# A twelve-sublayer decoder: the end of the first mixture of experts moved into the stages of the block behind it, and the opening transfers staged

## The reference, cut to what matters

```python
x = _layernorm(x + _L0_attn_ref(x, gate_w, gate_b, w1, b1, w2, b2))       # 8 experts, top 2, gelu, 128 -> 512 -> 128
x = _layernorm(x + _L0_xattn_ref(x, ctx_1024, Wq, bq, Wk, bk, Wv, bv))    # one head, keys and values from ctx
x = _layernorm(x + _L0_ffn_ref(x, W1, b1, W2, b2))                        # weights rounded to -1, 0 or 1, 128 -> 512 -> 128
...
```

## Time and profile before

| | us |
|---|---|
| median of 3 runs | 3722.18 (3711.93 to 3723.31) |
| the profiled execution | 3689.48 |
| its span, first to last instruction | 3687.8 |
| PE busy | 2935.0 (80%) |
| DVE busy | 2176.2 (59%) |
| ACT busy | 1819.6 (49%) |
| POOL busy | 1825.7 (50%) |
| mean granted TensorE clock | 0.895 |

### The profile page before, as it was taken

One profiled execution on the slowest core, in us unless ns is written; L12 is line 12 of the kernel. 1 busy time (PEld: TensorE's weight loads), 2 busy tenths in 40 slices (PEclk: granted clock), 3 DMA queues, 4 the chain that ended last, 5 costly groups with the idle time before them and its releaser, 6 DMA issues. The chain is left out here.

```text
span 3687.8 us, 83881 instructions
## 1 busy us (share of the span) xinstructions
PE 2935.0 (80%) x28814; PEld 2040.0 (55%) x28814; DVE 2176.2 (59%) x5986; ACT 1819.6 (49%) x3516; POOL 1825.7 (50%) x1735
## 2 busy tenths in 40 slices
PE   2688873998888789963529997997999869995895
PEld 1677762775555556642315664664444536664784
DVE  2111133756878668863247886877898678884124
ACT  0333331844555556630216665776466677662342
POOL 3533254434777645526465554664033655553335
PEclk9998986999999889985559998998999889996997
DMA  8566652120010121114621112221000011222675
GB/s 284 160 184 182 185 161 70 45 8 25 30 46 37 41 74 70 71 45 118 169 57 51 58 54 85 77 90 62 1 1 1 1 30 56 72 69 84 204 218 149
DMA packets 325000, 315.45 MB, mean 86 GB/s; under 512 B 111316, under 2 KB 244853, under 8 KB 324472
## 3 DMA queue, kind: packets, MB, share of 16 engines
q1 hardware_dynamic: 283080, 261.98, 23.4%
q0 software_dynamic: 16384, 33.59, 3.1%
q10 hardware_dynamic: 25264, 16.40, 1.5%
HBM read 167.28 MB, written 60.69 MB: 62 GB/s over the span
## 5 line engine op out<-in xcount | busy, mean ns | idle before, releaser
L1054 PE MATMUL moe_first_out_ps<-moe_first_expert_w,moe_first_hid 128*128 128x128 f32 x1360 | 214.9, 311 | 84.5 <-ACT moe_first_hid L1098 63.5
L1098 ACT ACTIVATE moe_first_hid<-moe_first_hid_ps,moe_first_expert_w 128x256 f32<-128x256 f32 x340 | 139.0, 472 | 260.2 <-PE moe_first_hid_ps L1043 141.7
L908 DVE TENSOR_TENSOR moe_first_tile_y<-moe_first_out_ps,moe_first_expert_w 128x256 f32<-128x256 f32 x85 | 36.1, 425 | 368.9 <-PE moe_first_out_ps L1054 187.7
L1054 PEld LDWEIGHTS moe_first_out_ps<-moe_first_expert_w,moe_first_hid 128*128 128x128 f32 x1360 | 191.4, 211 | 102.9 <-issue 42.3
L1117 POOL DMA_INDIRECT slot_x<-x_tok,moe_first_slots x128 | 124.6, 974 | 119.7 <-DMA slot_x<-blank 49.3
L1131 POOL DMA_INDIRECT moe_first_token_y<-slot_y,moe_first_slots x128 | 123.5, 965 | 107.9 <-issue 67.8
L1043 PE MATMUL moe_first_hid_ps<-moe_first_tile_xT,moe_first_expert_w 128*128 128x256 f32 x680 | 171.4, 397 | 1.9 <-issue 1.4
L1813 POOL TENSOR_TENSOR causal_k_blocks<-causal_k_T,headmask 128x1024 f32<-128x1024 f32 x64 | 121.3, 1898 | 99.4 <-PE causal_scores L1423 93.7
L1813 POOL TENSOR_TENSOR alibi_k_blocks<-alibi_k_T,headmask 128x1024 f32<-128x1024 f32 x64 | 121.3, 1897 | 94.0 <-PE alibi_scores L1423 90.0
L1813 POOL TENSOR_TENSOR full_k_blocks<-full_k_T,headmask 128x1024 f32<-128x1024 f32 x64 | 120.8, 1898 | 83.7 <-PE full_scores L1423 78.8
L1098 ACT ACTIVATE moe_last_hid<-moe_last_hid_ps,moe_last_expert_w 128x256 f32<-128x256 f32 x212 | 86.7, 471 | 140.2 <-PE moe_last_hid_ps L1043 110.0
(11 more groups left out here) (561 smaller groups left out, 8902.0 us busy)
## 6 DMA issues: line engine op xcount, KB each, us to landing
moe_first_expert_w<-in_L_attn_experts SPq DMA_DIRECT2D x85, 578.0 KB
moe_last_expert_w<-in_L_ffn_experts SPq DMA_DIRECT2D x53, 578.0 KB
moe_first_tile_x<-slot_x SPq DMA_DIRECT2D x85, 128.0 KB
slot_y<-moe_first_tile_y SPq DMA_DIRECT2D x85, 128.0 KB
slot_x<-blank ACTq DMA_DIRECT2D x2, 4992.0 KB, 35.9
L_ffn_tile_x<-slot_x SPq DMA_DIRECT2D x32, 256.0 KB
slot_y<-L_ffn_tile_y SPq DMA_DIRECT2D x32, 256.0 KB
moe_last_tile_x<-slot_x SPq DMA_DIRECT2D x53, 128.0 KB
```

Of the source, the lines that this page charges most:

```text
L908: dve.tensor_tensor(y_out[:, q, :, :], out_bank[q][:, 0:SLOT_TILE].rearrange("p (s d) -> p s d", s=SPAN), over(wall[:, j % RING, 2 * FF + ...
L1054: last = pe.matmul(out_bank[j % 2][:, D * s:D * s + D], hid[:, j % 2, b, TILE * s:TILE * s + TILE], wall[:, j % RING, FF + D * b:FF + D * ...
L1098: act.activation(hid[:, j % 2, b, :], hid_bank[b // 2][:, SLOT_TILE * (b % 2):SLOT_TILE * (b % 2) + SLOT_TILE], gelu, bias=wall[:, j % RIN ...
```

## The change

Two things are done.

**The opening.** `SLOT_TILES` becomes (23, 39, 39), so that the first part's slot tensor has 23 tiles, which that part needs; `L_ffn` takes the two of 39 instead. `x_T` and `x_tok` are loaded in three pieces of 16, 32 and 16 tiles, each piece of both forms together, and SP holds back the second and third until slot tensor 0 is cleared. ACT clears slot tensor 0 first, and 1 and 2 each after the exponential of the part before and once that piece of `x_T` has landed.

**The end of the first sublayer.** With `hand_over` the `moe` generator closes its block after the last `evict`, keeps `slots`, `weights`, `token_y` and the tail's buffers, and hands a `Late` object to `chained`. The chunks 12 to 15 (m = 0 to 3) are gathered, summed, normalised, transposed and copied in stages of the joined block, one chunk to three steps. The clearing of the first sublayer's semaphores moves behind the joined block; one barrier stays between the blocks.

```diff
-SLOT_TILES = (39, 39, 23)
+SLOT_TILES = (23, 39, 39)
+LOAD_TILES = (16, 32, 16)
...
+        for n, tiles in enumerate(LOAD_TILES):
+            some, cols = slice(first, first + tiles), slice(TILE * first, TILE * (first + tiles))
+            if n == 1 and hold_for_clearing:
+                sp.wait_ge(self.cleared[0], 16)
+            sp.dma_start(self.x_T[:, cols], self.dram["x_T"][:, cols]).then_inc(self.T_loaded[n], 16)
+            sp.dma_start(self.x_tok[:, some, :], rows[:, some, :]).then_inc(self.tok_loaded[n], 16)
+            first += tiles
...
@@ moe, ACT
                 if net.at == 0:
                     net.await_columns(act, 0)
-                    net.clear_slots(act)
+                    net.clear_slots(act, 0)
...
+                    if net.at == 0 and part + 1 < parts:
+                        net.await_columns(act, part + 1)
+                        net.clear_slots(act, part + 1)
...
@@ moe, the block's end
-        late = chunks[-1]
+        last_chunks = chunks[-1]
+        late = [] if hand_over else last_chunks
...
+        def late_gpsimd(pool):
+            def rows(c):
+                m, third = divmod(c, 3)
+                if m < len(last_chunks):
+                    gather(pool, FIRST + m, ((0, 1), (2,), (3,))[third])
+            def inverse_std(c):
+                m, third = divmod(c, 3)
+                if third == 0 and m < len(last_chunks):
+                    tail.inverse_std(pool, FIRST + m)
+            return [(-5, rows), (-1, inverse_std)]
...
+            return [(-2, weighted_sum), (0, normalise)]
...
+                    if m:
+                        pe.wait_ge(host.xT_copied, c - 2)
+                    tail.transpose(pe, FIRST + m, bank)
+            return [(0, transpose)]
...
+                    tail.copy_transposed(act, FIRST + m, bank)
+            return [(0, copy)]
...
@@ single_head
+                if before and c >= before.first:
+                    pe.wait_ge(before.tail.xT_copied, c + 1)
...
+            def turn_normed(c):
+                if before:
+                    pe.wait_ge(before.tail.xT_copied, before.copied_by(c + 3))
+                tail.transpose(pe, c, xT_bank)
...
+                if before and c >= before.first:
+                    pool.wait_ge(before.tail.normed, c + 1)
```

More of the change, by code:

```diff
@@ L40 @@
 LN_EPS = 1e-5
[L41 removed]
+IN_CHAIN = (2, 3, 10)
 BIG = 3.0e38
@@ L150, in __init__, with load_stream @@
         self.sublayer_sems = []
-    def load_stream(self, sp):
-        half, tiles = TOKENS // 2, TILES // 2
-        for n in range(2):
-            sp.dma_start(self.x_T[:, half * n:half * n + half], self.dram["x_T"][:, half * n:half * n + half])\
-                .then_inc(self.T_loaded[n], 16)
-        rows = self.dram["x"].rearrange("(t p) d -> p t d", p=128)
-        for n in range(2):
-            sp.dma_start(self.x_tok[:, tiles * n:tiles * n + tiles, :], rows[:, tiles * n:tiles * n + tiles, :])\
-                .then_inc(self.tok_loaded[n], 16)
+    def load_stream(self, sp, hold_for_clearing=False):
+        rows = self.dram["x"].rearrange("(t p) d -> p t d", p=128)
+        first = 0
+        for n, tiles in enumerate(LOAD_TILES):
[5 more added lines that the diff above has]
+            first += tiles
     def load_constants(self, sp):
@@ L684, in moe @@
     tile_of = [(n, m) for n, count in enumerate(NTS) for m in range(count)]
-    def halves(part):
-        half = TILES // 2
-        return range(origin[part] // half, (origin[part] + sizes[part] - 1) // half + 1)
     def by_expert(t, k):
@@ L767, in moe, with combine, gather @@
         after_tile = {due(c): c for c in range(CHUNKS) if due(c) is not None}
-        late = chunks[-1]
+        last_chunks = chunks[-1]
+        late = [] if hand_over else last_chunks
+        def combine(dve, c):
+            p, part = c % 2, part_of[c]
+            dve.wait_ge(gathered[p], 16 * PER * top * (c // 2 + 1))
+            if c >= 2:
+                dve.wait_ge(tail.normed, c - 1)
+            for r in range(top):
+                if r:
+                    dve.wait_ge(half_summed, c + 1)
+                for k in range(PER):
+                    t = PER * c + k - origin[part]
+                    base_row = net.x_tok[:, PER * c + k, :] if r == 0 else tail.r[:, p, k, :]
+                    last = dve.scalar_tensor_tensor(tail.r[:, p, k, :], y_in[:, p, k, r, :], weights[:, part, r, t:t + 1],
+                                                    base_row, ALU.mult, ALU.add)
+                last.then_inc(tail.summed if r == top - 1 else half_summed, 1)
+            tail.moments(dve, c)
+        def gather(pool, c, some):
+            p, part = c % 2, part_of[c]
+            if c == chunks[part][0] and 0 in some:
+                for q in range(2):
+                    pool.wait_ge(y_stored[q], 16 * ((reach[part + 1] + 1 - q) // 2))
+            if c >= 2 and 0 in some:
+                pool.wait_ge(tail.summed, c - 1)
+            for k in some:
+                for r in range(top):
+                    t = PER * c + k - origin[part]
+                    pool.indirect_dma_start(y_in[:, p, k, r, :], None, slot_y[part][0:NTS[part] * SLOT_TILE, :],
+                                            bass.IndirectOffsetOnAxis(slots[:, part, r, t:t + 1], 0))\
+                        .then_inc(gathered[p], 16)
         with nc.Block() as block:
@@ L1004, in route @@
                 def route(part):
-                    for n in halves(part):
-                        net.await_columns(pe, n)
+                    net.await_columns(pe, part)
                     if part:
@@ L1143, in _ @@
                     pool.wait_ge(net.cleared[part], 16)
-                    for n in halves(part):
-                        net.await_rows(pool, n)
+                    net.await_rows(pool, part)
                     pool.wait_ge(planned, 2 * part + 2)
@@ L1916, in finish, with __init__, copied_by @@
     tail.all_stored(sp)
+class Late:
+    def __init__(self, tail, first, vector, tensor, scalar, gpsimd):
+        self.tail, self.first = tail, first
+        self.vector, self.tensor, self.scalar, self.gpsimd = vector, tensor, scalar, gpsimd
+    def copied_by(self, step):
+        return self.first + min(CHUNKS - self.first, max(0, (step + 2) // 3))
 class Flow:
@@ L1937, in chained @@
     yield
-    flows = [next(sublayers[0])]
+    late = next(giver) if giver else None
+    if giver:
+        net.nc.all_engine_barrier()
+        net.at += 1
+    flows = [sublayers[0].send(late) if giver else next(sublayers[0])]
     for sublayer in sublayers[1:]:
@@ L1949, in _ @@
         def _(dve):
-            staged(joined(flows[0].vector(dve), flows[1].vector(dve)), AHEAD, BEHIND)
+            staged(joined(flows[0].vector(dve), flows[1].vector(dve)) + (late.vector(dve) if late else []), AHEAD, BEHIND)
         @block.sync
```

128 lines of the change are left out of this document (67 added, 61 removed).

## The result

| | before | with the change |
|---|---|---|
| median (8 runs each) | 3717.06 us (3700.65 to 3734.51) | 3686.22 us (3679.78 to 3694.07) |
| ratio | 1 | 0.9921, 95% interval 0.9906 to 0.9936 |
| the profiled execution | 3689.48 us | 3685.81 us |

The change saves about 29 us by the ratio and 31 by the two medians; the forecast was 56, with a range of 3642 to 3696. So the tiles are compared with the second profile.

A forecast was written before the change was run, and what follows sets the result against it. It took two meeting opening chains (POOL's scatters, PE's late routing) and one chain at the first sublayer's end as bounds. Opening 27 plus end 29 (55 less 26 given back) made 56: 3722.2 - 56 = 3666 us, range 3642 to 3696.

The forecast's parts named there:

- the rule weighed: Joined block's gathers: DVE's two-port mode could lock POOL from writing descriptors, 68 us lost, total near 3734; not adopted.
- its routing takes 7 us: Opening: the second piece of `x_T` lands at about 31 us and PE then routes that part in 7 us.
- nothing in the trace tells what causes the drag: Opening: PE's unexplained slow third routing, 24.6 us before; kept or gone, first turn 19.7 or 33.7 us earlier, middle 27.
- the slower rival: Opening: second routing drags beside POOL's scatters, 0.65 us per instruction, first turn at about 298, time 3885; chance 0.04.
- can be turned at about 72: Opening, chain of POOL's scatters: first slot tile fetched at 69.2 us, turned at about 72, 33.7 us earlier.
- the clearing of slot tensor 2 costed at nothing: Opening: its rest may be in flight at the first tiles, 5 MB in 15 us, ending by about 75; no cost.
- the delays add: Joined block: PE's and POOL's delays do not overlap, 45 us given back instead of 26, time 3685; chance 0.12.
- Start: Joined block: first maxima come 16.6 us after its start instead of 11.8, giving back 5 us.
- never idle: Joined block, steps 1 to 6: POOL always busy, some 6.9 us a step, giving back 12 us.
- PE's stands: Joined block, steps 3, 6, 9: PE waits 4 to 5 us at late transposes; two counted half, 7 us given back.
- POOL held up by DVE: Joined block: each of 32 gathers 0.41 us slower, 13 us more given back, 43 in all, time 3679; chance 0.06.
- The opening gains nothing: Opening: drag starts sooner or second routing is delayed and drags, first turn stays at 105, time 3693; chance 0.06.

The follow-up runs named there:

- the second profile: The kernel before, unchanged, run and profiled again on the first kind of chip: 3712.86 us, profiled span 3711.1 us.
- change_again: The change, unchanged, timed again on a chip of the second kind: 3502.45 us, ratio 0.9905 to the kernel before on that chip.
- before_third: The kernel before, unchanged, profiled again on a chip of the second kind: 3541.14 us.

## Why the prediction was right or wrong

**Right**: faster, and inside the range. The time is less close than it looks: the gain is half of the forecast's 56, 3686 lies outside the forecast's own range of 3650 to 3680, and 5 us of the way come from the first median of the kernel before (3722 from 3 runs, 3717 from 8). The own range takes 22 us for the end at its lowest where its terms say 10; with 10 it would have reached 3692. The first scatter at 27 (27.3). The slot tiles unchanged. Gathers at 0.94 to 1.18 us in the joined block, where the kernel before has up to 1.156: they were not slowed, so the rule weighed (the Trainium skill, SBUF — State Buffer, section "SBUF: two separate sides") has no row here either. The joined block's earlier start, 55.0 forecast, is 59.3: it starts 1.6 us behind the last bias, not 5.6.

**The opening, 27 forecast, 10.6 measured.** The step that failed is "its routing takes 7 us". It took 43.4 in the change's profile on the first kind of chip. I had refused to name a cause of the drag ("nothing in the trace tells what causes the drag") and costed the second routing at full pace all the same, though the change puts it beside POOL's scatters; the slower rival had just this mechanism. It was priced far too high, since the drag ends with POOL's scatters, and does not run on for each instruction. The trace of before hinted at it. Behind the 32nd scatter at 90.27, the last in the earlier trace rows, POOL issues four of the second part, and the dragging matmuls stop 2.9 us behind the last of them, at 98.22:

```profile
95.33 0.96 POOL L1117 DMA_INDIRECT slot_x<-x_tok,moe_first_slots  x1 [0.30 <-issue]
```

On the second kind of chip "7 us" was exact (7.00), and another step failed: "can be turned at about 72" and the clearing of slot tensor 2 costed at nothing. It is issued from 43.45 on and lands at 84.4. From 50 to 80 us the DMA share is 1.05, that is all 16 engines are busy, and the rows that the first tile needs lie behind it. The last of its 32 scatters, the fetch of its rows and its turn in `change_again`:

```profile
67.09 0.96 POOL L1132 DMA_INDIRECT slot_x<-x_tok,moe_first_slots  x1 [0.30 <-issue]
...
73.60 0.39 SPq L987 DMA_DIRECT2D moe_first_tile_x<-slot_x  x1
...
79.83 0.69 PE L1044 MATMUL moe_first_turn_ps<-ident,moe_first_tile_x 128*128 128x128 f32 x2 [19.85 <-DMA moe_first_tile_x<-slot_x]
```

From scatter to fetch are 6.5 us and from fetch to turn 6.2. In `before_third`, whose clearings have landed by then, both are 2.3 (90.99, 93.24, 95.49). That makes the turn at 79.8 instead of 72: 7.8 us that the forecast did not have. There is no drag to remove from the kernel before there, so its first turn is at 95.5.

**The end, 29 forecast, 14.4 measured.** The give-back is 44.9 instead of 26, which is the rival "the delays add" (45). That rival's time, 3685, is nearly the measured one, but that is luck: it has the opening at 27. By the terms of the end, on the first kind of chip:
- Start: 5 forecast, 9.6 measured. On the second kind it is 5.9; DVE's late start is the rest.
- POOL "never idle": wrong. It waits 34.1 us for DVE. Half of the gathers, left out, took 7.2 us out of the steps, where I had 12 for POOL's whole load; so the size may be near, and the path is another: it runs over POOL's late inverse deviation to DVE's normalising and PE's transposes.
- PE's stands: 7 forecast for them (two halves and one whole of "4 to 5 us" are 8 to 10), "POOL is late anyway, so I count half". They do not lie in POOL's shadow. The three long steps have 15.5, 14.4 and 11.5 us, 26 us over three steps of 5.1 together, and spreading the stages and a bank of their own took 9.5 and 8.8 us out of the steps. The cause is a chain: PE's last item of a step waits for rows of that same step, DVE normalises them only behind POOL's inverse deviation, and the late transposes share a bank with the attention's.

**The rivals**: "POOL held up by DVE" fell. "The opening gains nothing" was half right, with the drag sooner; the opening still gained 10 us.

## What to carry to other kernels

Work that is moved into another loop's steps needs a whole step of distance from its producer on every engine and a buffer (here a PSUM bank) of its own; with both given, POOL's added load is the smaller part of what it cost. (Of 41.0 us given back, distance took away 16.1 and the bank 8.8, so that at most 16 are left for POOL. In the close spacing half of its gathers was worth 13, since their time lay on the same chain.) A stall that the trace gives no reason for is not a number to be carried over: look at what the other engines do from its first to its last instruction, and do not put new work there. And a transfer that is "still in flight" is not free when the first thing that is waited for moves by the same DMA engines.

## What was not expected of the hardware

- On one kind of chip PE and DVE start instructions late while POOL issues indirect transfers one after another: pairs of routing matmuls 1.4 to 2.8 us apart, DVE's ready maxima 9.5 us late, slot tiles at 476.1 us instead of 363.1. On two other chips the same program shows nothing of it, and takes 180 us less. Between the chips most of this difference (113 us) lies in the 85 slot tiles. The drag does not begin with the transfers: 45 and 71 routing matmuls ran at full pace beside POOL's scatters before it set in. Each chip was used in one set of runs only, so it is not shown that the chip itself makes the kind, and not something else that held at the time.
- Which path of POOL's transfers the two kinds differ in stays open; no run could tell it. The profile's list of DMA queues has two that carry instructions (packets of 0.01 and 0.02 MB). In the change's profile on the first kind none of their packets falls between 36 and 80 us, and three do on the second kind, but engines that start fewer instructions need fewer, so that is no proof. The Trainium skill (Runtime: NRT & Kernel Launch, section "Instruction fetch mechanics") says that the engines' instructions are fetched ahead in blocks and that the cost of this is mostly hidden; the drag would be an exception to it, if fetching is its cause.
- A wait that the profile calls "issue" or "remote" here stood for a real delay of up to 9.5 us. In the first profile of the kernel before the drag that is made of such waits is 24.6 us long, and it was the most valuable line of the opening.
